# One attention and FFN layer in split fp32: joining the first score tiles of plain and latent keys in heads two to four of each group

## The chip, the cores and the metric

One core of one Trainium2 chip. The time is the device time of one execution of the whole program in microseconds; lower is better. TensorE is the matmul engine, VectorE, ScalarE and GpSimd work on tiles, and SyncE (SP) issues the transfers between the chip's memory (HBM) and the on-chip buffer SBUF. PSUM holds what TensorE writes.

## The reference

An attention layer and an FFN layer on an input x of shape (1, 1024, 512), both ahead of a residual addition and behind a layer norm:

```
q  = rope(x @ w_q)          # 32 heads of 128
k  = rope(x @ w_k)          # 8 key heads, each for 4 query heads
v  = x @ w_v                # 8
lk = rope((x @ w_lq) @ w_lk)   # 32 latent key heads, from a latent of 128
lv = x @ w_lv                  # 32
attn = causal_softmax(q @ k.T / sqrt(128)) @ v
lat  = causal_softmax(q @ lk.T / sqrt(128)) @ lv
x = x + attn @ w_o + lat @ w_lo
x = x + x_norm @ W.T + b + LoRA mixed by a router
```

Each head therefore has two attentions with the same queries: one over the plain keys of its group, one over latent keys of its own.

## The kernel before

All large products are made three times in a split form: each operand is kept as a rounded high part and the remainder (`hi` and `lo`), and `mm3` adds lo x hi, hi x lo and hi x hi into one PSUM tile. ScalarE makes the high part (a copy that rounds), VectorE or GpSimd the remainder (a subtraction).

The work is 8 groups (`g`) of 4 heads (`hh`, 0 to 3). A head has four passes `w`, in the order of `WINDOWS`: pass 0 is plain keys and queries 0 to 511 (chunk `c` = 0), pass 1 plain keys and queries 512 to 1023, pass 2 and pass 3 the same with latent keys. A pass with c = 0 has 4 blocks of 128 keys, one with c = 1 has 8. A block is a slot `s`. In each slot TensorE does, in this order:

- the score tiles of the NEXT pass whose place `TILE_SLOTS[w][t]` is this slot (tile `t` has 128 queries and all keys up to its diagonal, so 128 to 512 keys for c = 0 and 640 to 1024 for c = 1);
- a `piece` if `pieces_of` has one: a projection (Q and K of the next head or group, latent keys `LK`, latent values `LV`, values `V`) or a tile of the output projection (`OUT0`, `OUT1`);
- the transposes of the probabilities of block s + 2 into `bankT`, then the product of block s with the values into `bankO`.

In the last slot it also transposes blocks 0 and 1 of the next pass. The order on every engine is written out by hand, and semaphores tie the engines. A score tile goes TensorE (`scores[t % 2]`), VectorE (`row_max`, which adds the mask, writes the scaled scores to `probs` and their maximum to `nmax`), ScalarE (`exp_tile`, in place, with the row sum in `rsum`), TensorE (transposes). A transposed block goes through ScalarE (`block_hi`, L887) and VectorE (`block_lo`, L1113). TensorE may not overwrite a `scores` buffer before its row maximum is done, nor `bankT[j % 2]` before `block_lo` of the block in it (L580 to L582).

A rotary piece (Q, K, LK) is copied by ScalarE into one of three buffers `rot` (`rope_take`), multiplied by the sines on VectorE (`rotate`, two instructions of 64 partitions, L1123 and L1124), multiplied by the cosines and added on GpSimd (`rope_add`), rounded by ScalarE (`rope_high`), and its remainder made on GpSimd (`rope_low`). The latent keys of a head have two pieces, chunk 0 and chunk 1, both in pass 0 of that head, slots 0 and 1. Tile t = 0 of pass 2 is made in pass 1, slot 1, and waits for the remainder of chunk 0. Tiles t = 0 of pass 0 (next head) are made in pass 3, slot 4.

SP fetches weights through two staging buffers in turn; the load of number n waits for the remainder of weight n - 2. It also stores the inverse row sums and loads them back spread over the partitions (`spread_inverses`) between the weight loads.

Of the kernel before, what the change touches and what calls it, by code (L numbers as in the profile page):

```python
# [46 lines left out]
def pieces_of(g, hh, w):  # L47
# [3 lines left out]
    if w == 0:  # L51
        return {0: ("LK", 0), 1: ("LK", 1), **({3: ("LV", 0)} if more else {})}
    if w == 1:
        if (g, hh) == FIRST:
            return {0: ("LV", 1), 2: ("LV", 2), 5: ("LV", 3)}
        out = {s: ("OUT1", n) for n, s in enumerate((1, 2, 4, 7) if next_group else (1, 3, 5, 7))}
        ahead = {3: ("K", 0), 5: ("K", 1), 6: ("V", 0)} if next_group else {}
        return {**({0: ("LV", 1)} if more else {}), **out, **ahead}
# [18 lines left out]
def loads_of(g, hh):  # L77

    if (g, hh) == FINAL:
        return ["Wo", "Wlo"]  # L80
    if hh % 2:
        return (["Wk", "Wv"] if hh == GROUP - 1 else []) + ["Wq", "Wo", "Wlo", "Wlk"]
    if (g, hh) == (KVH - 1, GROUP - 2):
        return ["Wq", "Wo", "Wlo", "Wlk"]
    return ["Wq", "Wlv0", "Wo", "Wlo", "Wlk", "Wlv1"]


ROPE = ("Q", "K", "LK")
# [68 lines left out]
def attn_ffn_kernel(nc, x_in, w_q, w_k, w_v, w_o, w_lq, w_lk, w_lv, w_out_latent, W, b, A, B, router_W, router_b,  # L157
                    cos_in, sin_in, mask_in, ident_in, pick_in, out, inverses):
    with ExitStack() as ctx:
# [19 lines left out]
        KT = pair("KT", [P, S])  # L179
        LKT = pair("LKT", [P, S])  # L180
# [19 lines left out]
        nmax = sb("nmax", [P, 2, TPC])  # L200
        rsum = sb("rsum", [P, 2, TPC])
# [37 lines left out]
        Wlv0, Wlv1 = [[h[:, :, k * HD:(k + 1) * HD] for h in Wlv] for k in range(2)]  # L239

# [84 lines left out]
        def tiles_made(g, hh, w):  # L325

            return TPC * (unit_no(g, hh, w) + 1)
# [32 lines left out]
        def tile_bank(n, c, width):  # L360
            return scores[n % 2][:, 0, 0:width] if c == 0 else scores[n % 2][:, :, 0:width // 2]

# [37 lines left out]
        def _(sp):  # L400
# [39 lines left out]
            def group_of_heads(g, last):  # L440
                for hh in range(GROUP):
# [18 lines left out]
                    if more:  # L460
                        if hh == GROUP - 1:
                            fetch("Wk", "Wv", "Wq")
                        else:
                            fetch("Wq", "Wlv0" if "Wlv0" in loads_of(g, hh) else "Wo")
                    if not more:
# [10 lines left out]
                        sp.wait_ge(x_ready, n_piece(g, hh, 0, 0))  # L476
# [34 lines left out]
        def _(pe):  # L511
# [50 lines left out]
            def score_tile(no, parity, head, kind, c, t):  # L562

                if not (isinstance(no, int) and no < 2):
                    pe.wait_ge(row_maxed, no - 1)
# [3 lines left out]
                query = both(QT, ALL, head % 2, slice(i * P, (i + 1) * P))  # L569
                if c == 0:  # L570
# [7 lines left out]
            def transpose_block(g, hh, w, j):  # L578
# [4 lines left out]
                for t in range(max(0, j - TPC * c), TPC):  # L583
                    if j == 0:
                        pe.wait_ge(exped, tiles_made(g, hh, w) - TPC + t + 1)
                    at = p_offset(c, t) + j * P
                    mm = pe.transpose(bankT[j % 2][:, t * P:(t + 1) * P],  # L587
                                      probs[c][:, at:at + P], ident[:, :])
# [16 lines left out]
            def piece(g, hh, w, s, name, n):  # L605
                bank_x_taken(pe, g, hh, w, s)
                bank = piece_bank(g, hh, w, s)
                if name == "LK":
                    pe.wait_ge(w_lo, key_load(g, hh) + 1)
                    mm = mm3(bankX[:, :], both(Wlk, ALL, ALL), both(lqT, ALL, slice(n * CH, n * CH + CH)), True, True)  # L610
                elif name == "LV":
# [40 lines left out]
            def group_of_heads(g, last):  # L652
                for hh, w, more in windows(g, last):
# [8 lines left out]
                    for s in range(BLOCKS[w]):  # L662
                        if more or w < NW - 1:
                            for t in range(TPC):
                                if TILE_SLOTS[w][t] != s:
                                    continue
                                no = tiles_made(g, hh, w) + t
                                if t == 0 and w in (1, 2):

                                    pe.wait_ge(rope_lo, rope_no(g, hh, "LK", w - 1) + 1)  # L670
                                if t == 0 and w == 3:

                                    pe.wait_ge(rope_lo, rope_no(g, hh, "Q", 0) + 1)
                                if t == 0 and w == 0:

                                    pe.wait_ge(rope_lo, rope_no(g, hh, "LK", 0))
                                if t == 1 and w == 0:
                                    pe.wait_ge(x_free, frees_ahead(g, hh, 0))
                                if t == 1 and w == 2:
                                    pe.wait_ge(x_free, frees_ahead(g, hh, 2))  # L680
                                score_tile(no, t % 2, nhh, WINDOWS[nw][0], WINDOWS[nw][1], t)
# [45 lines left out]
            for t in range(TPC):  # L727
                if t == 1:
                    pe.wait_ge(x_free, 3)
                score_tile(t, t % 2, 0, 0, 0, t)  # L730
# [81 lines left out]
        def _(act):  # L812
# [60 lines left out]
            def exp_tile(no, c, t):  # L873

                act.wait_ge(row_maxed, no + 1)
                act.activation(prob_tile(c, t), prob_tile(c, t), ACT.Exp, bias=nmax[:, c, t:t + 1], scale=-1.0,  # L876
                               accum_out=rsum[:, c, t:t + 1]).then_inc(exped, 1)
# [12 lines left out]
            highs = [{(0, 3): ("LK", 0), (1, 0): ("LK", 1), (3, 1): ("Q", 0), (3, 3): ("Q", 1)} for _ in range(GROUP)]  # L890
            highs[GROUP - 1].update({(1, 5): ("K", 0), (2, 0): ("K", 1)})

            def group_of_heads(g, last):
                for hh, w, more in windows(g, last):
                    nw, nhh = (w + 1) % NW, hh + (w == NW - 1)
                    kind, c = WINDOWS[w]
                    for s in range(BLOCKS[w]):
# [4 lines left out]
                        early = s + 2 < BLOCKS[w] and name in ("", "LK", "OUT0", "OUT1")  # L902
                        if early:
                            block_hi(g, hh, w, s + 2)
                        if more or w < NW - 1:
                            for t in range(TPC):
                                if TILE_SLOTS[w][t] == s:
                                    exp_tile(tiles_made(g, hh, w) + t, WINDOWS[nw][1], t)
# [596 lines left out]
```

## Time and profile before

| | |
|---|---|
| Time, median of 3 runs | 2036.36 us (2036.19 to 2036.54) |
| Time of the profiled execution | 2036.75 us |
| Its span, first to last instruction | 2035.0 us |
| Busy: TensorE, VectorE, ScalarE, GpSimd | 2018.2, 1457.1, 1203.7, 889.9 us |
| Mean granted TensorE clock | 0.998 |

Busy time is the time in which at least one instruction of the engine runs. Matmuls overlap, so their durations add up to more than the span; the pace of TensorE is the distance between starts. The granted clock is 1.0 at full speed. A row of the order of time gives the start, the duration, the engine, the line, what is written and read and the shape, and in brackets the idle time before it with what ended it.

### The profile page before, as it was taken

To read this page: it belongs to the slowest core of one execution; us is meant where nothing else is said; L and a number is where in the kernel's file an instruction comes from. 1 tells how busy PE (TensorE), PEld (TensorE's weight loads), DVE (VectorE), ACT (ScalarE), POOL (GpSimd) and SP (SyncE) were. 2 spreads that over 40 slices of the span, in tenths; PEclk is the share of its full clock that TensorE was granted. 3 is DMA by queue.
4 is the path that set the end of the run, shared out by engine and by line. 5 is a ranking of instruction groups with operands and counts; after the bars stand their busy time and mean duration, and the time that the engine had idled before them with its cause. 6 is when DMAs were issued, how large, how long until landed. Compare 5 with 4: busy or idle time off the path is not lost.

```text
span 2035.0 us, 33416 instructions
## 1 busy us (share of the span) xinstructions
PE 2018.2 (99%) x11716; PEld 1753.1 (86%) x11716; DVE 1457.1 (72%) x2884; ACT 1203.7 (59%) x2505; POOL 889.9 (44%) x684
## 2 busy tenths in 40 slices
PE   8999999999999999999999999999999999999989
PEld 7888888888888888888888888888888888888877
DVE  7677776776777767777677776777776776777777
ACT  4666556565565656666566565666566565565651
POOL 5444544444443454444534454444544444443422
PEclk9999999999999999999999999999999999999999
DMA  3111111111111111112111111111111111111031
GB/s 108 47 34 44 48 28 38 34 49 37 38 39 39 33 44 37 44 28 49 33 44 37 39 39 28 49 34 44 48 28 41 32 49 39 37 39 38 23 68 42
DMA packets 101797, 83.78 MB, mean 41 GB/s; under 512 B 28152, under 2 KB 73848, under 8 KB 101632
## 3 DMA queue, kind: packets, MB, share of 16 engines
q1 hardware_dynamic: 101632, 81.65, 15.7%
q8 instruction: 95, 1.56, 0.3%
q14 instruction: 70, 0.57, 0.1%
HBM read 79.26 MB, written 2.36 MB: 40 GB/s over the span
## 4 chain that ended last, share of the span: by engine, by line
PE 97%; DVE 2%; ACT 1%; POOL 0%; issue 0%; DMA 0%; DVEq 0%; ACTq 0%
PE bankT L587 13%; PE scores L514 12%; PE scores L516 12%; PE scores L515 12%; PE bankX L514 9%; PE bankX L516 9%; PE bankX L515 9%; PE bankO L516 7%; PE bankO L515 7%; PE bankO L514 7%; PE scores L707 0%; PE scores L553 0%; DVE rot_half L1124 0%; DVE xnT_lo L1097 0%; ACT probs L876 0%
## 5 line engine op out<-in xcount | busy, mean ns | idle before, releaser
L815 ACT ACTIVATE PT_hi<-bankT 128x512 fp32r<-128x512 f32 (+2 forms) x640 | 337.5, 533 | 310.7 <-PE bankO L516 275.5
L1113 DVE TENSOR_TENSOR PT_lo<-bankT,PT_hi 128x512 fp32r<-128x512 f32 (+2 forms) x640 | 388.1, 607 | 175.7 <-ACT PT_hi L815 173.1
L876 ACT ACTIVATE probs<-probs,nmax 128x128 f32<-128x128 f32 (+7 forms) x512 | 393.9, 771 | 129.8 <-DVE nmax L1107 129.7
L1107 DVE CUSTOM_DVE_ANT_0 probs<-scores,mask 128x128 f32<-128x128 f32 (+7 forms) x512 | 379.2, 750 | 69.3 <-PE scores L516 68.0
L587 PE MATMUL bankT<-ident,probs 128*128 128x128 f32 x2304 | 382.7, 275 | 6.8 <-ACT probs L876 5.0
L587 PEld LDWEIGHTS bankT<-ident,probs 128*128 128x128 f32 x2304 | 279.6, 140 | 67.9 <-DVE PT_lo L1113 11.7
L1369 POOL TENSOR_TENSOR rot<-rot,cos 128x512 f32<-128x512 f32 x144 | 186.9, 1298 | 256.6 <-DVE rot_half L1124 256.6
L1363 POOL TENSOR_TENSOR OT_lo<-o_raw,OT_hi 128x512 fp32r<-128x512 f32 x63 | 98.3, 1560 | 319.9 <-ACT OT_hi L815 319.9
L815 ACT ACTIVATE OT_hi<-o_raw 128x512 fp32r<-128x512 f32 x128 | 146.7, 1146 | 139.7 <-DVE o_raw L1182 139.7
L1371 POOL TENSOR_TENSOR rot<-rot,rot_half 128x512 f32<-128x512 f32 x144 | 199.9, 1388 | 11.3
L1123 DVE TENSOR_TENSOR rot_half<-rot,sin 64x512 f32<-64x512 f32 x144 | 99.5, 691 | 135.3 <-ACT rot L815 132.3
L815 ACT ACTIVATE rot<-bankX 128x512 f32<-128x512 f32 x140 | 82.9, 592 | 101.9 <-PE bankX L516 101.9
L1124 DVE TENSOR_TENSOR rot_half<-rot,sin 64x512 f32<-64x512 f32 x144 | 140.6, 976 | 2.0
L514 PE MATMUL scores<-LKT_hi,QT_lo 128*128 128x384 f32 (+5 forms) x384 | 138.7, 361 | 0.2 <-POOL LKT_lo L1363 0.2
L1363 POOL TENSOR_TENSOR QT_lo<-rot,QT_hi 128x512 fp32r<-128x512 f32 x64 | 91.8, 1435 | 103.5 <-ACT QT_hi L815 103.5
L514 PE MATMUL bankO<-PT_hi,V_lo 128*128 128x512 f32 (+2 forms) x320 | 136.4, 426 | 0.0
L514 PE MATMUL bankO<-PT_hi,LV_lo 128*128 128x512 f32 (+2 forms) x320 | 136.2, 426 | 0.0
L1140 DVE TENSOR_TENSOR acc<-bankX,acc 128x512 f32<-128x512 f32 x133 | 91.7, 690 | 61.1 <-PE bankX L516 61.1
L514 PE MATMUL scores<-KT_hi,QT_lo 128*128 128x384 f32 (+5 forms) x384 | 133.0, 346 | 0.3 <-DVE nmax L1107 0.3
L516 PE MATMUL scores<-LKT_hi,QT_hi 128*128 128x384 f32 (+5 forms) x384 | 131.8, 343 | 0.0
L515 PE MATMUL scores<-LKT_lo,QT_hi 128*128 128x384 f32 (+5 forms) x384 | 131.5, 342 | 0.0
L516 PE MATMUL scores<-KT_hi,QT_hi 128*128 128x384 f32 (+5 forms) x384 | 131.4, 342 | 0.0
(304 smaller groups left out, 5334.0 us busy)
## 6 DMA issues: line engine op xcount, KB each, us to landing
inv_b<-inverses SPq DMA_DIRECT2D x128, 256.0 KB, 3.9
stage<-in_L_attn_w_q SPq DMA_DIRECT2D x32, 256.0 KB, 4.8
stage<-in_L_attn_w_lv SPq DMA_DIRECT2D x32, 256.0 KB, 2.9
stage<-in_L_attn_w_o SPq DMA_DIRECT2D x32, 256.0 KB, 3.5
stage<-in_L_attn_w_lo SPq DMA_DIRECT2D x32, 256.0 KB, 2.6
acc<-in_L_attn_hidden_states SPq DMA_DIRECT2D x8, 256.0 KB, 4.9
stage<-in_L_attn_w_k SPq DMA_DIRECT2D x8, 256.0 KB, 5.0
stage<-in_L_attn_w_v SPq DMA_DIRECT2D x8, 256.0 KB, 5.0
```

The costliest lines, as they stand in the source:

```text
L514: pe.matmul(place, left[1], right[0], start=start, stop=False)
L515: pe.matmul(place, left[0], right[1], start=False, stop=False)
L516: return pe.matmul(place, left[0], right[0], start=False, stop=stop)
L587: mm = pe.transpose(bankT[j % 2][:, t * P:(t + 1) * P], probs[c][:, at:at + P], ident[:, :])
L815: return act.activation(place, src, ACT.Copy)
L876: act.activation(prob_tile(c, t), prob_tile(c, t), ACT.Exp, bias=nmax[:, c, t:t + 1], scale=-1.0, accum_out=rsum[:, c, t:t + 1]).then_inc( ...
L1107: dve.tensor_tensor_reduce(place, src, tile_view(mask[:, S - width:S], c), -SCALE, -MASKED, ALU.add, ALU.min, nmax[:, c, t:t + 1]).then_in ...
L1113: dve.tensor_tensor(pt_place(1, hh, w, j), bankT[j % 2][:, block_columns(c, j):CH], f32(pt_place(0, hh, w, j)), ALU.subtract).then_inc(pt_ ...
L1124: dve.tensor_tensor(rot_half[HALF:HD, half, :], rot[0:HALF, slot, :], sin[0:HALF, t], ALU.mult)\
L1363: return pool.tensor_tensor(place, src, f32(hi), ALU.subtract)
L1369: pool.tensor_tensor(rot[:, slot, :], rot[:, slot, :], cos[:, chunk(n)], ALU.mult).then_inc(rope_cos, 1)
L1371: pool.tensor_tensor(rot[:, slot, :], rot[:, slot, :], rot_half[:, half, :], ALU.add).then_inc(rope_sum, 1)
```

## The change

In heads hh = 1, 2 and 3 of each group (24 of the 32 heads) the score tile t = 0 of pass 0 (plain keys) and tile t = 0 of pass 2 (latent keys) have the same queries, 0 to 127, and 128 keys each. They are now made in one `mm3` of 256 columns in pass 3, slot 4 of the head before. For this:

- plain and latent keys lie in one tensor `keys_T` of [128, 2, 1024], so that one operand can read 128 columns of each.
- the latent piece of chunk 0 is made one head ahead, as `LKA` in pass 1, slot 4 (hh = 0 to 2), from a weight `Wlk` that is loaded, rounded and split earlier (pass 1). Its rotation on VectorE comes two slots later, behind the row maximum of tile t = 3. ScalarE rounds it in pass 2, slot 0, after a wait for the last score tile that reads the old keys; GpSimd makes its remainder between those of `Wo` and `Wlo`.
- the row maximum and the exponential of the latent tile move with it; its probabilities lie in a tile of their own, `probs_ahead`, until pass 2, and its maxima and sums in a third set.
- head 0 of each group keeps both tiles and both pieces where they were.
- on GpSimd, the remainder of Q's chunk 0 in pass 3 now waits until VectorE has rotated Q's chunk 1.

```diff
     if w == 0:
-        return {0: ("LK", 0), 1: ("LK", 1), **({3: ("LV", 0)} if more else {})}
+        return {**({0: ("LK", 0)} if hh == 0 else {}), 1: ("LK", 1), **({3: ("LV", 0)} if more else {})}
...
+        latent = {4: ("LKA", 0)} if hh < GROUP - 1 else {}
+        return {**({0: ("LV", 1)} if more else {}), **out, **ahead, **latent}
...
-        return (["Wk", "Wv"] if hh == GROUP - 1 else []) + ["Wq", "Wo", "Wlo", "Wlk"]
+        return (["Wk", "Wv"] if hh == GROUP - 1 else []) + ["Wq", "Wlk", "Wo", "Wlo"]
...
-    return ["Wq", "Wlv0", "Wo", "Wlo", "Wlk", "Wlv1"]
+    return ["Wq", "Wlk", "Wlv0", "Wo", "Wlo", "Wlv1"]
...
+def tiles_at(g, hh, w, s):
+    if w == NW - 1 and (g, hh) == FINAL:
+        return []
+    to = (g, hh, w + 1) if w < NW - 1 else (*divmod(g * GROUP + hh + 1, GROUP), 0)
+    tiles = []
+    for t in range(TPC):
+        if TILE_SLOTS[w][t] == s:
+            if t or w != 1 or hh == 0:
+                tiles.append((*to, t))
+            if t == 0 and w == NW - 1 and to[1]:
+                tiles.append((*to[:2], 2, 0))
+    return tiles
...
-        KT = pair("KT", [P, S])
-        LKT = pair("LKT", [P, S])
+        keys_T = pair("keys_T", [P, 2, S])
...
+        KT, LKT = [[h[:, kind, :] for h in keys_T] for kind in range(2)]
...
# SP
-                            fetch("Wq", "Wlv0" if "Wlv0" in loads_of(g, hh) else "Wo")
+                            fetch("Wq", "Wlk")
...
-                    if hh == GROUP - 1 or "Wlv0" in loads_of(g, hh):
-                        fetch("Wo")
-                    fetch("Wlo")
+                    if hh == GROUP - 1:
+                        fetch("Wlk")
+                    if "Wlv0" in loads_of(g, hh):
+                        fetch("Wlv0")
+                    fetch("Wo", "Wlo")
                     spread_inverses(g, hh, 2)
-                    fetch("Wlk")
...
# TensorE, score_tile
+                if (w, t) == (0, 0) and hh:
+                    mm3(scores[0][:, 0, 0:2 * P].rearrange("p (k n) -> p k n", k=2), query,
+                        both(keys_T, ALL, ALL, slice(0, P)), True, True).then_inc(scored, 2)
+                    return
...
# ScalarE
+                        if w == 1 and s == (5 if hh == GROUP - 1 else 2) and more:
+                            act.wait_ge(x_ready, n_piece(g, hh, 0, 1))
+                            fetched(g, hh, "Wlk", Wlk)
...
+                            if s == 0 and hh < GROUP - 1:
+                                act.wait_ge(scored, tiles_made(g, hh, 3))
+                                rope_high(rope_no(g, hh, "LKA", 0), rope_no(g, hh, "LKA", 0) % RING, LKT[0][:, 0:CH])
...
-                        if w == 3 and s == 5 and more:
-                            fetched(g, hh, "Wlk", Wlk)
...
# VectorE
-                        if here.get(s - 1, ("", 0))[0] == "LK":
-                            piece(g, hh, w, s - 1, *here[s - 1], piece_bank(g, hh, w, s - 1))
+                        for behind_by, name in ((1, "LK"), (2, "LKA")):
+                            at = s - behind_by
+                            if here.get(at, ("", 0))[0] == name:
+                                piece(g, hh, w, at, *here[at], piece_bank(g, hh, w, at))
...
# GpSimd
                     if w == 1 and more:
                         fetched_low(g, hh, "Wq", Wq)
+                        if hh < GROUP - 1:
+                            fetched_low(g, hh, "Wlk", Wlk)
...
                             fetched_low(g, hh, "Wlv0", Wlv0)
+                        if hh < GROUP - 1:
+                            rope_add(rope_no(g, hh, "LKA", 0), rope_no(g, hh, "LKA", 0) % RING, 0)
...
                         fetched_low(g, hh, "Wo", Wo)
+                        if more and hh < GROUP - 1:
+                            rope_low(rope_no(g, hh, "LKA", 0), rope_no(g, hh, "LKA", 0) % RING, LKT, (ALL, chunk(0)))
                         fetched_low(g, hh, "Wlo", Wlo)
...
                     if w == 3 and more:
+                        pool.wait_ge(rope_half, rope_no(g, hh, "Q", 1) + 1)
                         rope_low(rope_no(g, hh, "Q", 0), rope_no(g, hh, "Q", 0) % RING, QT, q_at(0))
```

## Rows read from the trace of the kernel before

**Rows 1.** The page: busy time, share of the span and instructions of each engine.

```profile
PE 2018.2 (99%) x11716; PEld 1753.1 (86%) x11716; DVE 1457.1 (72%) x2884; ACT 1203.7 (59%) x2505; POOL 889.9 (44%) x684
```

**Rows 2.** The page: shares of the chain that ended last.

```profile
PE 97%; DVE 2%; ACT 1%; POOL 0%; issue 0%; DMA 0%; DVEq 0%; ACTq 0%
```

**Rows 3.** The waits, all engines: total us, times, longest.

```profile
PEld scores L514 <- POOL LKT_lo L1363: 11.6, 32, 0.9
```

**Rows 4.** Order of time, TensorE, pass 3, slots 3 and 4, around tile t = 0.

```profile
583.86 0.39 PE L516 MATMUL bankO<-PT_hi,LV_hi 128*128 128x512 f32 x1
...
584.54 0.28 PE L515 MATMUL scores<-KT_lo,QT_hi 128*128 128x256 f32 x1
584.66 0.28 PE L516 MATMUL scores<-KT_hi,QT_hi 128*128 128x256 f32 x1
```

**Rows 5.** Order of time, TensorE, pass 0, slot 0.

```profile
594.00 0.39 PE L514 MATMUL bankX<-lqT_hi,Wlk_lo 128*128 128x512 f32 x1
...
594.70 0.38 PE L587 MATMUL bankT<-ident,probs 128*128 128x128 f32 x2
```

**Rows 6.** Windows in the last head: us, busy (instructions), granted clock, DMA share, GB/s.

```profile
1938.00:1943.00 5.00, 1.44 (x10) 0.97 (x9) 4.23 (x6) 3.10 (x7) 4.16 (x3) 1.00 0.08 28
1943.00:1949.80 6.80, 6.48 (x21) 4.98 (x21) 4.19 (x9) 2.27 (x3) 3.86 (x4) 0.50 0.03 2
```

**Rows 7.** Order of time, TensorE, pass 1, slots 0 and 1.

```profile
608.79 0.40 PE L516 MATMUL bankO<-PT_hi,V_hi 128*128 128x512 f32 x1
...
609.10 0.33 PE L514 MATMUL scores<-LKT_hi,QT_lo 128*128 128x128 f32 x1
...
609.77 0.40 PE L515 MATMUL bankX<-Wo_lo,OT_hi 128*128 128x512 f32 x1
```

**Rows 8.** Order of time, GpSimd, ahead of the latent tile t = 0.

```profile
607.74 1.30 POOL L1363 TENSOR_TENSOR LKT_lo<-rot,LKT_hi 128x512 fp32r<-128x512 f32 x1
```

**Rows 9.** Order of time, VectorE, start of pass 0.

```profile
593.38 0.69 DVE L1113 TENSOR_TENSOR PT_lo<-bankT,PT_hi 128x512 fp32r<-128x512 f32 x1 [0.43 <-ACT PT_hi L815]
```

**Rows 10.** Order of time, VectorE, last head, pass 0.

```profile
1936.67 0.69 DVE L1123 TENSOR_TENSOR rot_half<-rot,sin 64x512 f32<-64x512 f32 x1
...
1938.09 1.22 DVE L1107 CUSTOM_DVE_ANT_0 probs<-scores,mask 128x1024 f32<-128x1024 f32 x1
```

**Rows 11.** Order of time, VectorE, end of pass 1, start of pass 2.

```profile
678.55 0.69 DVE L1107 CUSTOM_DVE_ANT_0 probs<-scores,mask 128x512 f32<-128x512 f32 x1 [0.59 <-PE scores L516]
...
680.12 0.69 DVE L1140 TENSOR_TENSOR acc<-scores,acc 128x512 f32<-128x512 f32 x1 [0.87 <-PE scores L516]
681.25 0.69 DVE L1113 TENSOR_TENSOR PT_lo<-bankT,PT_hi 128x512 fp32r<-128x512 f32 x1 [0.44 <-ACT PT_hi L815]
...
682.92 0.17 DVE L1200 RECIPROCAL rinv<-rsum 128x4 f32<-128x4 f32 x1
```

**Rows 12.** Order of time, TensorE, pass 2, tile t = 2.

```profile
683.86 0.48 PE L514 MATMUL scores<-LKT_hi,QT_lo 128*128 128x448 f32 x1
684.17 0.36 PE L515 MATMUL scores<-LKT_lo,QT_hi 128*128 128x448 f32 x1
```

**Rows 13.** Order of time, GpSimd, end of pass 1, the same head.

```profile
677.27 1.28 POOL L1363 TENSOR_TENSOR Wlv_lo<-stage,Wlv_hi 128x512 fp32r<-128x512 f32 x1 [4.04 <-ACT Wlv_hi L815]
```

**Rows 14.** Order of time, VectorE, pass 0, slot 2.

```profile
603.36 1.68 DVE L1124 TENSOR_TENSOR rot_half<-rot,sin 64x512 f32<-64x512 f32 x1
```

**Rows 15.** Order of time, GpSimd, the same moment.

```profile
602.81 1.67 POOL L1371 TENSOR_TENSOR rot<-rot,rot_half 128x512 f32<-128x512 f32 x1
```

**Rows 16.** Order of time, VectorE, start of the program.

```profile
16.77 0.38 DVE L1057 BATCH_NORM_AGGREGATE inv_b<-inv_b 128x2 f32<-128x6 f32 x4
17.18 0.89 DVE L1064 TENSOR_SCALAR inv_b<-inv_b 128x4 f32<-128x4 f32 x1
```

**Rows 17.** Order of time, GpSimd, the same moment.

```profile
16.75 1.29 POOL L1363 TENSOR_TENSOR Wlv_lo<-stage,Wlv_hi 128x512 fp32r<-128x512 f32 x1 [2.46 <-ACT Wlv_hi L815]
```

**Rows 18.** DMA issues: KB each, median us from issue to landing.

```profile
stage<-in_L_attn_w_lv SPq DMA_DIRECT2D x32, 256.0 KB, 2.9
```

More of the change, by code:

```diff
@@ L81, in loads_of, with number_tiles @@
     if hh % 2:
-        return (["Wk", "Wv"] if hh == GROUP - 1 else []) + ["Wq", "Wo", "Wlo", "Wlk"]
+        return (["Wk", "Wv"] if hh == GROUP - 1 else []) + ["Wq", "Wlk", "Wo", "Wlo"]
     if (g, hh) == (KVH - 1, GROUP - 2):
-        return ["Wq", "Wo", "Wlo", "Wlk"]
-    return ["Wq", "Wlv0", "Wo", "Wlo", "Wlk", "Wlv1"]
-ROPE = ("Q", "K", "LK")
+        return ["Wq", "Wlk", "Wo", "Wlo"]
+    return ["Wq", "Wlk", "Wlv0", "Wo", "Wlo", "Wlv1"]
[11 more added lines that the diff above has]
+    return tiles
+def number_tiles():
+    order = [(*FIRST, 0, t) for t in range(TPC)]
+    for g in range(KVH):
+        for hh in range(GROUP):
+            for w in range(NW):
+                for s in range(BLOCKS[w]):
+                    order += tiles_at(g, hh, w, s)
+    last, ahead = [None, None], {}
+    for at in order:
+        ahead[at] = last[at[3] % 2]
+        last[at[3] % 2] = at
+    return {at: no for no, at in enumerate(order)}, ahead
+TILE_NO, AHEAD_IN_SCORES = number_tiles()
+ROPE = ("Q", "K", "LK", "LKA")
 X_BEFORE = 10
@@ L610, in piece @@
                     mm = mm3(bankX[:, :], both(Wlk, ALL, ALL), both(lqT, ALL, slice(n * CH, n * CH + CH)), True, True)
+                elif name == "LKA":
+                    pe.wait_ge(w_lo, load_no(g, hh, "Wlk") + 1)
+                    mm = mm3(banksX[bank], both(Wlk, ALL, ALL), both(lqT, ALL, slice(0, CH)), True, True)
                 elif name == "LV":
@@ L901, in group_of_heads @@
                                       piece_bank(g, hh, w, s))
-                        early = s + 2 < BLOCKS[w] and name in ("", "LK", "OUT0", "OUT1")
+                        early = s + 2 < BLOCKS[w] and name in ("", "LK", "LKA", "OUT0", "OUT1")
                         if early:
                             block_hi(g, hh, w, s + 2)
[L905 to L908, printed above, removed]
-                        if name in ("Q", "K"):
+                        for at in tiles_at(g, hh, w, s):
+                            exp_tile(*at)
+                        if name in ("Q", "K", "LKA"):
                             rope_take(n_piece(g, hh, w, s), rope_no(g, hh, name, n), rope_no(g, hh, name, n) % RING,
@@ L1363, in subtract, with rope_add @@
                 return pool.tensor_tensor(place, src, f32(hi), ALU.subtract)
-            def rope_add(no, slot, n, place=None):
-                half = n if place is None else place
+            def rope_add(no, slot, n):
+                half = no % 2
                 pool.wait_ge(rope_half, no + 1)
@@ L1389, in ropes @@
             def ropes(g, hh, name, places, at):
-                for n in range(2):
+                halves = range(1 if hh and name == "LK" else 0, 2)
+                for n in halves:
                     rope_add(rope_no(g, hh, name, n), rope_no(g, hh, name, n) % RING, n)
-                for n in range(2):
+                for n in halves:
                     rope_low(rope_no(g, hh, name, n), rope_no(g, hh, name, n) % RING, places, at(n))
@@ L1421, in group_of_heads @@
                         rope_add(*k_no[1], 1)
+                        fetched_low(g, hh, "Wlk", Wlk)
                     if w == 1 and more:
```

116 lines of the change are left out of this document (61 added, 55 removed).

## Prediction

> **What bounds the kernel now.** I read the busy shares first, then the chain, then the waits, and then the order of instructions over one head. TensorE is busy 99% of the span and VectorE 72% [rows 1]; the chain that ended last is TensorE for 97% [rows 2]. So a change pays only by what it takes from TensorE's own stream, or from the gaps in it. Gaps are few. The one that this change touches is the weight load of the first latent score tile, which waits for LKT_lo in all 32 heads, 11.6 us in total [rows 3], mostly under the matmul that still runs. In the order of time the reader should look at the distance between starts, not at the durations, because matmuls overlap. A 256-column matmul advances by 0.115 us (584.54 to 584.66); the three 128-column ones before it by 0.11 each (0.68 from 583.86, less 0.23 for the matmul that starts there and 0.115) [rows 4]; a 512-column one advances by 0.23 us (594.00 to 594.70 is three) [rows 5]. A 128-column matmul is therefore paced by something other than its columns, and doubling the columns is nearly free. All of this is at a granted clock of 1.0; one stretch, in the last head, is at 0.5 [rows 6].
>
> **The sum, part by part.** The base is the profiled execution: span 2035.0 us, its time 2036.75, so 1.75 lie around the span; the median of the three runs is 2036.36, 0.39 below it. I subtract from the median.
>
> (a) The latent tile t = 0 leaves pass 1 in 24 heads. The last matmul ahead of it starts at 608.79, the second matmul behind it at 609.77 [rows 7]. Without the tile two steps of 0.23 us lie between: 0.46. The tile costs 0.98 - 0.46 = 0.52 us, its wait included. The wait: LKT_lo ends at 609.04 [rows 8] and the tile starts at 609.10.
>
> (b) The plain tile t = 0 becomes three 256-column matmuls. Before, 583.86 to the second matmul of t = 1 at 584.54 is 0.68 us [rows 4]. After: 0.23, three of 0.115 and one of 0.115 give 0.69. Cost 0.01. So (a) and (b) save 0.51 x 24 = 12.2 us. The trace has no operand in two runs of 128 columns; the bounds are 0 and a pace of twice 0.11, that is 3 x 0.105 = 0.32 us per head. I take 0, nearest to the 256-column rows, which differ in the stride alone. The Trainium skill ("TensorE: Matmul & The Clock Gate", Back-to-back issue gap) gives a warm gap of N/2.4 + 2.5 ns: 56 ns at 128 columns and 109 at 256. By that two tiles apart would cost as much as one joined tile, and the joining would save nothing; the trace's 0.11 us at 128 columns speaks against it.
>
> (c) The key piece of chunk 0 (three 512-column matmuls, 0.70 us [rows 5]) moves from pass 0 slot 0 to pass 1 slot 4 of the head before. The TensorE work is the same, but in pass 0 it was cover. Behind it stands the transpose group that overwrites bankT0, and it waits for PT_lo, which runs from 593.38 for 0.69, to 594.07 [rows 9]. TensorE would now come to it at 594.00 instead of 594.70. A start 0.06 behind the releaser (as 609.10 behind 609.04) is 594.13, so 0.13 late. The tile of (a) shows that a wait costs somewhat more than its late start: 0.52 us for three steps of 0.11 leaves 0.19, though it started only 0.08 late (609.10 against 608.79 + 0.23). I take 0.16 us in 24 heads: 3.8 us lost; bounds 0 and 0.25.
>
> (d) VectorE. The rotation of the moved piece (two instructions of 0.69 [rows 10]) goes behind the last row maximum of pass 1. There VectorE is free from 679.25 until 680.12 [rows 11]. Rotation 679.28 to 680.70, the addition of the output tile until 681.31 (0.61 from start to start), so PT_lo starts 0.06 late against 681.25. From there everything to the row maximum of the next pass is back to back, and TensorE's tile t = 2 already waits for that: its first step takes 0.31 us (683.86 to 684.17) where a 448-column step, between those of 256 and 512 columns, takes some 0.2 [rows 12]. So 0.06 x 24 = 1.4 us lost. In the 15 heads that round both a moved piece and a value half Wlv0 in pass 1, GpSimd's Wlv_lo now starts later; before it ended at 678.55 [rows 13], 0.7 us ahead of where the rotation would begin. ScalarE takes the new piece first (0.6 us) and TensorE puts it 0.2 later, so in a count with that shift it ends about 679.45, and the rotation starts at 679.49. I add 0.05 x 15 = 0.8; bounds 0 and 1.0 each. The added row maximum and exponential of 128 columns only move from pass 1 to pass 3 slot 4, where VectorE and ScalarE wait for TensorE.
>
> (e) GpSimd's multiplication and addition for the moved piece (1.3 us each) now run from about 680.8 to 683.5, over the reciprocal at 682.92 [rows 11], which reads and writes SBUF. What can be held? A rotation on VectorE took 1.68 instead of 0.69 us while a GpSimd addition ran to 604.48 [rows 14, 15]; a 4-element TENSOR_SCALAR from 17.18 took 0.89 us and ended with GpSimd's instruction at 18.04, but four BATCH_NORM_AGGREGATE beside the same one took 0.38 together [rows 16, 17]. No reciprocal in the trace overlaps one. Bounds: 0, or held to about 683.46, which is some 0.35 us for the row maximum and for TensorE behind it. I take 0. The Trainium skill ("SBUF — State Buffer", Who interferes with whom) has two-input instructions from SBUF and copy, cast and tensor_scalar as those that contend with GpSimd; the rows agree for the first and the last, and it does not name the reciprocal.
>
> (f) New waits. GpSimd waits for the second rotation of Q before QT_lo, about 0.6 us later, but then runs 1.3 instead of 1.7 us, done near 583.6 against about 584.1 for the tile (0.23 behind 583.86 [rows 4]): nothing. ScalarE waits in pass 2 for the last score tile, then rounds the keys (0.64 us); its next instruction needed a transpose behind that tile anyway, and the last exponential moves by 0.6 us where 1 us was free: nothing; beyond that, each tenth costs 2.4 us. The Wlk load moves ahead on SP, and its rounding (0.3) and GpSimd's remainder (0.5) into pass 1; the first latent value half and both output weights load one place later. They land some 3 us after issue (the value half's row [rows 18]) and are used 5 us later or more, except Wlv0, in (d). Nothing.
>
> (g) The last head. There is no other work on TensorE between passes, so it stands still behind the exponentials. Its 1,024-column row maximum stood behind the rotation of chunk 0 (1936.67, maximum at 1938.09), then PT_lo of the next pass behind a second rotation and ScalarE's rounding of the same keys [rows 10]. Without them the maximum starts 1.0 us earlier, and the transposes that ended the standstill near 1943.2 start near 1941.4: 1.8, of which 0.6 is already in (c). Add 0.4 for the longer wait at the latent tile. 1.6 us gained. Then the clock: granted 0.50 for 6.8 us from 1943.0, behind five us in which it was busy for 1.44 [rows 6]. TensorE now waits about 2.5 us in all there. I take it that the clock stays at 2.4 GHz; what it gives back is half of 6.8 less about 1.4 us of waits, 2.7 us. Bounds 0 and 2.7.
>
> Sum: -12.2 + 3.8 + 1.4 + 0.8 - 1.6 - 2.7 = -10.5 us: 2036.36 - 10.5 = 2025.9, say **2026** (with the clock down, 2028.6).
>
> **Rivals.** *The reciprocal is held* (e): 24 x 0.35 = +8.4, 2034.3: no measurable change. For it the TENSOR_SCALAR, against it the BATCH_NORM_AGGREGATE. *The joined tile is no cheaper* (b): 24 x 0.32 = +7.7, 2033.6. For it only that such an operand is nowhere in the trace. *The rotation meets Wlv_lo* (d), which ends on the other side: if that GpSimd instruction starts a few tenths later, or if the load of Wlv0 lands late, the rotation is held for its whole length, 1.0 us, and PT_lo and the row maximum with it, in 15 heads: +15, 2041. It cancels the gain from 0.7 us in each of them and is measurably slower from 1.0, its whole price. For it: the gap that I work out is 0.04 us. Against it: a small overlap costs only itself, and SP can issue this load some 7 us before use. *Other cover is lost* ((c) and (f) at their upper bounds, a tenth or two in 24 heads): 2031 to 2036.
>
> **How the numbers follow.** A measurement tells this kernel from itself within about 0.2%, 4.1 us. Forecast 0.62 (its own range 2022 to 2031), all faster; a gain above it 0.05, if (c) and (d) cost nothing (2020); reciprocal 0.11 and joined tile 0.04, no change; lost cover 0.09, split 0.04 faster and 0.05 no change; rotation 0.09 (with a little of the other losses beside it, which its whole price needs), 0.08 slower and 0.01 no change. Faster 0.71, same 0.21, slower 0.08. For eight in ten I leave out what lies under 2020.5 and over 2036.5.
>
> **What the profile after would show.** 72 joined matmuls of 256 columns at a pace of 0.115 us; no LKT tile of 128 columns in those heads; a wait of the transposes for PT_lo in pass 0 of some 0.15 us in 24 heads; the step of t = 2 in pass 2 at 0.35 to 0.4 us; a reciprocal of 0.17 us; one rotation in pass 1 of 0.69 twice; a clock of 1.0 near the end. The distance from head to head should shrink by about 0.3 us. Wrong would be a reciprocal or a rotation of over 1 us there, or a wait for QT_lo or exponentials that is not there now.

## The result, and the profile after

The changed kernel takes 2044.47 us (median of 6 runs, 2042.87 to 2045.78); the kernel before, on the same chip, 2036.28 (2035.65 to 2036.54). The ratio is 1.0038, with a 95% interval of 1.0028 to 1.0048: slower by 8.2 us, where 10.5 us less were forecast. The profiled execution has a span of 2044.0 us against 2035.0. Its own time is 2045.78, the slowest of the six, so what follows explains 9.0 us where the medians differ by 8.2.

The page of the changed kernel: busy time by engine, the chain that ended last (its line is quoted whole), and the one group that is new among the costliest.

```profile
PE 2021.3 (99%) x11644; PEld 1747.7 (86%) x11644; DVE 1432.6 (70%) x2884; ACT 1206.3 (59%) x2505; POOL 871.1 (43%) x684
...
PE 97%; DVE 2%; issue 0%; ACT 0%; DMA 0%; SPq 0%; DVEq 0%; ACTq 0%
PE scores L559 12%; PE bankT L637 12%; PE scores L561 12%; PE scores L560 12%; PE bankX L559 9%; PE bankX L561 9%; PE bankX L560 9%; PE bankO L561 7%; PE bankO L559 7%; PE bankO L560 7%; DVE o_raw L1242 1%; PE scores L598 0%; ACT probs L931 0%; DMA stage<-in_L_attn_w_q 0%; DVE probs L1149 0%
...
L559 PE MATMUL bankO<-PT_hi,V_lo 128*128 128x512 f32 (+2 forms) x320 | 136.4, 426 | 6.0 <-DVE o_raw L1242 6.0
```

72 matmuls are gone [rows 1], and TensorE is still busy 99% of the span. Busy time alone would have hidden the loss. What is new is VectorE's o_raw (line 1242) in the chain, and idle time of TensorE ahead of the first product with V. Its waits say the same (total us, times, longest); in the kernel before there is no wait of TensorE for o_raw at all, and the wait for the latent keys had 11.6 us in 32 places [rows 3].

```profile
PEld bankT L637 <- DVE PT_lo L1173: 16.0, 50, 1.0
PEld scores L559 <- POOL keys_T_lo L1423: 2.8, 8, 0.4
PE bankO L559 <- DVE o_raw L1242: 6.0, 24, 0.3
```

**The loss in pass 0.** The order of time in slot 0 of pass 0, second head of a group (start, duration; PE is TensorE, DVE VectorE), in the changed kernel:

```profile
597.76 0.69 DVE L1173 TENSOR_TENSOR PT_lo<-bankT,PT_hi 128x512 fp32r<-128x512 f32 x1 [0.44 <-ACT PT_hi L870]
598.24 0.31 PE L561 MATMUL scores<-keys_T_hi,QT_hi 128*128 128x320 f32 x1
598.37 0.68 DVE L1242 TENSOR_TENSOR o_raw<-bankO,inv_b 128x512 f32<-128x512 f32 x1
598.51 0.44 PE L637 MATMUL bankT<-ident,probs 128*128 128x128 f32 x2
599.20 0.47 PE L559 MATMUL bankO<-PT_hi,V_lo 128*128 128x512 f32 x1 [0.25 <-DVE o_raw L1242]
```

and the two rows of the kernel before that answer to the third and the fifth (the transposes are in [rows 5]):

```profile
593.99 0.68 DVE L1182 TENSOR_TENSOR o_raw<-bankO,inv_b 128x512 f32<-128x512 f32 x1
...
594.83 0.48 PE L514 MATMUL bankO<-PT_hi,V_lo 128*128 128x512 f32 x1
```

The transposes were due 0.15 us behind the score matmul of 598.24 and start 0.12 later than that; by the ends it is 0.18 (598.95 is 0.40 behind the end of the score matmul at 598.55; before, 595.08 was 0.22 behind the end of the key piece at 594.86): the wait that the forecast had. Then comes a second one. The product overwrites bankO, which o_raw reads until 599.05. Before, o_raw ended at 594.67, when the key piece was just running out, and the product ended 0.23 us behind the transposes (595.31 against 595.08). Now it ends 0.72 behind them (599.67 against 598.95): 0.49 us of standstill. The moved piece had covered two waits, not one.

**The loss in pass 3.** TensorE's first product with Wo, in slot 2, needs OT_lo. It ends 0.47 us behind the end of the matmul ahead of it, in the kernel before 0.31, where the pace is 0.23. The cause lies 6 us earlier, in the order of time of all engines (ACT is ScalarE, POOL GpSimd):

```profile
633.29 0.63 ACT L870 ACTIVATE keys_T_hi<-rot 128x512 fp32r<-128x512 f32 x1
...
636.15 0.62 ACT L870 ACTIVATE Wlo_hi<-stage 128x512 fp32r<-128x512 f32 x1
636.84 1.28 POOL L1423 TENSOR_TENSOR Wlo_lo<-stage,Wlo_hi 128x512 fp32r<-128x512 f32 x1 [1.06 <-ACT Wlo_hi L870]
637.78 0.89 DVE L1183 TENSOR_TENSOR rot_half<-rot,sin 64x512 f32<-64x512 f32 x1 [2.90 <-ACT rot L870]
...
641.97 1.08 DVE L1250 TENSOR_TENSOR OT_lo<-o_raw,OT_hi 128x512 fp32r<-128x512 f32 x1 [0.69 <-ACT OT_hi L870]
642.80 0.40 PE L561 MATMUL bankO<-PT_hi,LV_hi 128*128 128x512 f32 x1
643.20 0.47 PE L559 MATMUL scores<-Wo_hi,OT_lo 128*128 128x512 f32 x1
```

The rounding of the moved keys stands on ScalarE ahead of the last two exponentials, these end later, and with them Wlo_hi and Wlo_lo. Wlo_lo now runs until 638.12, over the start of VectorE's rotation of Q, which takes 0.89 us. Before, Wlo_lo ended at 633.23, just as the rotation began, and the rotation took 0.69:

```profile
631.95 1.28 POOL L1363 TENSOR_TENSOR Wlo_lo<-stage,Wlo_hi 128x512 fp32r<-128x512 f32 x1 [1.98 <-ACT Wlo_hi L815]
633.17 0.69 DVE L1123 TENSOR_TENSOR rot_half<-rot,sin 64x512 f32<-64x512 f32 x1 [2.90 <-ACT rot L815]
...
638.17 0.40 PE L516 MATMUL bankO<-PT_hi,LV_hi 128*128 128x512 f32 x1
638.41 0.47 PE L514 MATMUL scores<-Wo_hi,OT_lo 128*128 128x512 f32 x1
```

PT_lo, o_raw, ScalarE's OT_hi and OT_lo follow the rotation one behind the other, so the 0.2 us arrive at the product.

**The books.** For every matmul I take the distance of its end from the end of the one ahead, less the usual distance for its width, and add up by place over 23 of the 24 heads, scaled to 24. In us:

| part | forecast | profile |
|---|---|---|
| latent tile gone, tiles joined | -12.2 | -11.7 |
| transposes wait for PT_lo, pass 0 | +3.8 | +4.5 |
| product with V waits for o_raw, pass 0 | not seen | +11.7 |
| first product with Wo, pass 3 | 0 | +5.1 |
| tile t = 2 of pass 2; Wlv_lo | +2.2 | +1.1 |
| last head: standstill and clock | -4.3 | -2.5 |
| start of the program | 0 | +0.8 |
| sum | -10.5 | +9.0 |

The spans differ by 9.0. What makes the last row but one is not shown. In this execution the clock was at 0.50 for 3.4 us from 15.9, which it was not in the execution of before; but the profiled execution of e10, with the same drop, ends its 251st matmul at 53.02 against 52.92 before, and that of e2, without a drop, at 53.55.

### The profile page after: what moved, and what is told of

Read it like the earlier page. It is cut to its first block, busy times and chain, and to the rows that moved or that the text cites. A ratio compares the mean times of both kernels' runs of the same rounds, so it can differ in the third digit from the quotient of the medians.

```text
span 2044.0 us, 33310 instructions
## 1 busy us (share of the span) xinstructions
PE 2021.3 (99%) x11644; PEld 1747.7 (86%) x11644; DVE 1432.6 (70%) x2884; ACT 1206.3 (59%) x2505; POOL 871.1 (43%) x684
## 4 chain that ended last, share of the span: by engine, by line
PE 97%; DVE 2%; issue 0%; ACT 0%; DMA 0%; SPq 0%; DVEq 0%; ACTq 0%
PE scores L559 12%; PE bankT L637 12%; PE scores L561 12%; PE scores L560 12%; PE bankX L559 9%; PE bankX L561 9%; PE bankX L560 9%; PE bankO L561 7%; PE bankO L559 7%; PE bankO L560 7%; DVE o_raw L1242 1%; PE scores L598 0%; ACT probs L931 0%; DMA stage<-in_L_attn_w_q 0%; DVE probs L1149 0%
## 5 line engine op out<-in xcount | busy, mean ns | idle before, releaser
L931 ACT ACTIVATE probs<-probs,nmax 128x256 f32<-128x256 f32 (+7 forms) x480 | 380.8, 796 | 120.4 <-DVE nmax L1167 120.2
L1167 DVE CUSTOM_DVE_ANT_0 probs<-scores,mask 128x256 f32<-128x256 f32 (+7 forms) x480 | 371.8, 781 | 100.0 <-PE scores L561 99.6
L559 PE MATMUL scores<-keys_T_hi,QT_lo 128*128 128x384 f32 (+5 forms) x744 | 264.0, 355 | 0.3 <-DVE nmax L1167 0.3
L561 PE MATMUL scores<-keys_T_hi,QT_hi 128*128 128x384 f32 (+5 forms) x744 | 256.4, 345 | 0.0
L560 PE MATMUL scores<-keys_T_lo,QT_hi 128*128 128x384 f32 (+5 forms) x744 | 256.3, 344 | 0.0
L1183 DVE TENSOR_TENSOR rot_half<-rot,sin 64x512 f32<-64x512 f32 x144 | 104.2, 723 | 135.8 <-ACT rot L870 132.8
L559 PEld LDWEIGHTS scores<-keys_T_hi,QT_lo 128*128 128x128 f32 x744 | 139.9, 188 | 24.7 <-DVE nmax L1167 10.4
L1423 POOL TENSOR_TENSOR keys_T_lo<-rot,keys_T_hi 128x512 fp32r<-128x512 f32 x80 | 103.6, 1294 | 125.9 <-ACT keys_T_hi L870 125.9
L560 PEld LDWEIGHTS scores<-keys_T_lo,QT_hi 128*128 128x128 f32 x744 | 140.0, 188 | 11.9
L561 PEld LDWEIGHTS scores<-keys_T_hi,QT_hi 128*128 128x128 f32 x744 | 139.7, 188 | 10.1
```

The costliest lines, as they stand in the source:

```text
L559: pe.matmul(place, left[1], right[0], start=start, stop=False)
L560: pe.matmul(place, left[0], right[1], start=False, stop=False)
L561: return pe.matmul(place, left[0], right[0], start=False, stop=stop)
L931: act.activation(tile_of(w, t), tile_of(w, t), ACT.Exp, bias=nmax[:, exp_sums(w), t:t + 1], scale=-1.0, accum_out=rsum[:, exp_sums(w), t:t ...
L1167: dve.tensor_tensor_reduce(place, src, tile_view(mask[:, S - width:S], c), -SCALE, -MASKED, ALU.add, ALU.min, nmax[:, exp_sums(w), t:t + 1 ...
L1183: dve.tensor_tensor(rot_half[0:HALF, half, :], rot[HALF:HD, slot, :], sin[HALF:HD, t], ALU.mult)
```

## Experiments

Each kernel is timed against the kernel before on its chip (2036.32, 2036.58 and 2036.88 us in the three groups); all stand beside the changed kernel's 2044.47. The changed kernel was not run again on those chips; the kernel before differs between them and its first chip (2036.28) by up to 0.6 us, so a difference of that size between groups says nothing. Of each edit the main lines are shown.

**e1_cover_back.** The key piece of chunk 1 moves from slot 1 to slot 0.

```diff
-        return {**({0: ("LK", 0)} if hh == 0 else {}), 1: ("LK", 1), **({3: ("LV", 0)} if more else {})}
+        keys = {0: ("LK", 1)} if hh else {0: ("LK", 0), 1: ("LK", 1)}
+        return {**keys, **({3: ("LV", 0)} if more else {})}
```

Not shown: four waits of SP and ScalarE for the last piece of pass 0 that follow it to its new place.

> The changed kernel, but in heads two to four of a group the one key piece that is left in pass 0 (chunk 1, three 512-column matmuls, 0.70 us) goes to slot 0 instead of slot 1. Theory A (lost cover): in the changed kernel TensorE stands still twice in slot 0 of pass 0, about 0.18 us for PT_lo ahead of the transposes and about 0.49 us ahead of the first product with V, which waits for o_raw to read out bankO. A piece in between covers both: 0.67 x 24 = 16 us less than the changed kernel's 2044.5, so 2028 to 2029, the wait for o_raw gone from the waits, and about 8 us less than the kernel before. Rival B (the loss lies in VectorE's and ScalarE's later work, the keys' rounding and rotation, and the stall in slot 0 only shows it): the time stays at 2042 to 2045, and the idle time turns up again ahead of the tiles of slot 1 or of the product in slot 1, which now lack the piece. Rival C (only half is covered, since slot 1 needs the piece as well): about 2036.

Measured: 2033.65 us (10 runs), ratio to before 0.9987 (0.9977 to 0.9996), 10.8 less than the changed kernel. Both waits are gone: in the order of time the piece starts at 595.37, the transposes at 596.06 and the product at 596.20, and the waits show none for o_raw. But a gain of 16 us was expected. One wait has grown: that of the transposes for the probabilities had 6.4 us in 7 places in the changed kernel and now has 11.0 in 30, while the one for PT_lo went from 16.0 in 50 to 10.5 in 26.

```profile
PEld bankT L638 <- ACT probs L932: 11.0, 30, 2.9
PEld bankT L638 <- DVE PT_lo L1174: 10.5, 26, 0.7
```

The order of time at the end of the pass shows where.

```profile
600.94 0.69 DVE L1184 TENSOR_TENSOR rot_half<-rot,sin 64x512 f32<-64x512 f32 x1
601.64 0.69 DVE L1185 TENSOR_TENSOR rot_half<-rot,sin 64x512 f32<-64x512 f32 x1
602.36 1.23 DVE L1168 CUSTOM_DVE_ANT_0 probs<-scores,mask 128x1024 f32<-128x1024 f32 x1
603.63 1.15 ACT L932 ACTIVATE probs<-probs,nmax 128x1024 f32<-128x1024 f32 x1 [1.75 <-DVE nmax L1168]
604.50 0.75 PE L638 MATMUL bankT<-ident,probs 128*128 128x128 f32 x4
```

Four transposes usually take 0.60 us to the last end. Here 0.75: the last waits for the exponential that ends at 604.78. The rotation came ahead of the row maximum again, and TensorE, with one piece less in this pass, is now faster than that chain. Theory A holds for the waits of slot 0; a part of the gain went to a wait that had been hidden (rival C in kind, but at the end of the pass, not in slot 1).

**e5_rotation_behind.** The same, with that rotation behind the row maximum.

```diff
-                        for behind_by, name in ((1, "LK"), (2, "LKA")):
+                        for behind_by, name in ((2 if hh else 1, "LK"), (2, "LKA")):
```

> The kernel with the cover back (chunk 1 in slot 0), and VectorE rotates that piece behind the row maximum of the fourth tile instead of ahead of it, in heads two to four. With the cover back that row maximum started at the end of the rotation, its exponential ended at 604.78 and TensorE's transposes of the next pass waited 0.15 us for it in each of 24 heads. Theory A: the last 3.5 us go, 2033.65 - 3.5 = about 2030. Rival: the sum of the moved keys on GpSimd comes later and holds something of VectorE instead, so nothing or a loss: 2033.5 or above.

Measured: 2028.26 us, ratio 0.9958 (0.9943 to 0.9973). That is 5.4 less than e1, where 3.5 were expected; the distances between matmul ends give 3.5 for the transposes, and the last head is 0.7 us shorter. The rest, about a microsecond, lies behind the last head, where the profiled execution of e1 is 1.4 us longer than this one. There e1 has a drop of the clock that this execution has not (window, busy by engine, granted clock, DMA share, GB/s):

```profile
1968.20:1971.60 3.40, 3.40 (x14) 3.00 (x15) 2.71 (x5) 2.23 (x3) 0.00 (x0) 0.50 0.00 0
```

From the start of one group of transposes to that of the next, the stretch takes 3.69 us in e1 (from 1968.11) and 2.34 at a clock of 1.0 here (from 1963.46). Why the clock falls there in the one and not in the other is open. So the cover, with nothing put in its place, is worth 16.2 us, with 1.5 to either side by the spread of the four runs: the whole 4.5 + 11.7 of the table.

**e8_piece_twice** and **e10_before_twice.** Work is added instead of moved: in slot 0 of pass 0 TensorE computes a key piece once more, 0.70 us, in the changed kernel (chunk 1) and as a control in the kernel before (chunk 0, `slice(0, CH)`, bank of slot 0).

```diff
+                        if (w, s) == (0, 0) and hh:
+                            bank_x_taken(pe, g, hh, 0, 1)
+                            pe.wait_ge(w_lo, key_load(g, hh) + 1)
+                            mm3(bankX[:, :], both(Wlk, ALL, ALL), both(lqT, ALL, slice(CH, S)), True, True)
```

> The changed kernel with work added: in slot 0 of pass 0 of heads two to four TensorE computes the key piece of chunk 1 once more (three 512-column matmuls, 0.70 us; the result is computed again in slot 1, where it is used). Theory A (TensorE stands still there for 0.18 + 0.49 us): the added work is free but for 0.03 us a head, so 2044 to 2046. Rival (the stall is not idle time of TensorE, or comes back elsewhere): 0.70 x 24 = 17 us more, 2061.

> The control for the piece computed twice: the kernel before the change, with its key piece of chunk 0 computed once more in slot 0 of pass 0 of heads two to four (three 512-column matmuls, 0.70 us). In that kernel TensorE does not stand still there, so theory A says the same added work that was free in the changed kernel costs its whole 0.70 x 24 = 17 us: 2053. Rival (such work is free in this place in any kernel, and proves nothing of a stall made by the change): 2037 to 2040.

Measured: 2044.69 us in the changed kernel, 0.2 more than without the added work (and 8.1 above the kernel before on its own chip, as against 8.2); 2053.65 in the kernel before, 16.8 more than its 2036.88 (ratio 1.0084, 1.0068 to 1.0099). The same 72 matmuls are free in the one and cost their whole 0.70 us a head in the other. This is the plainest evidence that TensorE stood still there for about 0.67 us in 24 heads, and only since the change. In the order of time the product now starts 0.14 us behind the transposes, as before the change:

```profile
597.85 0.39 PE L561 MATMUL bankX<-lqT_hi,Wlk_hi 128*128 128x512 f32 x1
598.08 0.38 PE L637 MATMUL bankT<-ident,probs 128*128 128x128 f32 x2
598.22 0.48 PE L559 MATMUL bankO<-PT_hi,V_lo 128*128 128x512 f32 x1
```

**e2_keys_later.** The rounding of the moved keys goes behind the weights: on ScalarE behind the first two blocks of pass 3, on GpSimd behind the sum of Q.

```diff
                     if w == 2 and more:
                         rope_add(rope_no(g, hh, "Q", 0), rope_no(g, hh, "Q", 0) % RING, 0)
+                        if hh < GROUP - 1:
+                            rope_low(rope_no(g, hh, "LKA", 0), rope_no(g, hh, "LKA", 0) % RING, LKT, (ALL, chunk(0)))
```

Not shown: the lines that take both roundings out of pass 2, and ScalarE's new ones.

> The changed kernel, but the high and low rounding of the moved keys (ScalarE, then GpSimd, chunk 0) goes from between the weights of pass 2 to behind them: on ScalarE behind the first two PT_hi of pass 3, on GpSimd behind the sum of Q's chunk 0. Theory A: in the changed kernel that rounding pushes Wlo_lo under the rotation of Q, which takes 0.89 instead of 0.69 us, and everything behind is late, until TensorE's first product with Wo in pass 3 waits about 0.24 instead of 0.08 us for OT_lo. The edit takes back 0.16 x 24 = 4 us: about 2040.5. Rival B: nothing, since the rounding's GpSimd part now lies beside VectorE's OT_lo and holds it, or the wait in pass 3 has another cause: 2044 or above, with OT_lo longer than 1.1 us.

Measured: 2047.52 us, 3.0 more. Rival B was right about the time, not about the way. The product with Wo has its pace back (it starts 0.24 us behind the matmul ahead). The loss is one slot later:

```profile
642.11 1.09 DVE L1250 TENSOR_TENSOR OT_lo<-o_raw,OT_hi 128x512 fp32r<-128x512 f32 x1 [0.67 <-ACT OT_hi L870]
642.22 2.10 POOL L1423 TENSOR_TENSOR keys_T_lo<-rot,keys_T_hi 128x512 fp32r<-128x512 f32 x1
643.90 0.97 DVE L1183 TENSOR_TENSOR rot_half<-rot,sin 64x512 f32<-64x512 f32 x1
644.88 0.68 DVE L1184 TENSOR_TENSOR rot_half<-rot,sin 64x512 f32<-64x512 f32 x1
...
646.35 0.55 PE L637 MATMUL bankT<-ident,probs 128*128 128x128 f32 x3 [0.24 <-DVE PT_lo L1173]
```

OT_lo is not held (1.09 us, as ever). GpSimd is, for 2.10 us instead of 1.29, and so reaches into the next rotation, which takes 0.97; the transposes wait for the PT_lo behind it.

**e3_both.** e1 and e2 together.

> Both edits together. If the two losses are separate places on TensorE's path, they add up: 16 + 4 = 20 us less than the changed kernel, about 2024.5, and 12 us (0.6%) less than the kernel before, which is about what the forecast gave for the change without its losses. If the stall in slot 0 of pass 0 only took over slack, the sum is smaller than its parts: 2028 or above.

Measured: 2035.16 us (10 runs), where 2024.5 were expected, and 1.5 more than e1 alone. The loss of e2 comes back beside the gain of e1, so it says only what e2 says.

**e6_wlo_ahead.** The second try at pass 3: nothing is moved on GpSimd, but ScalarE rounds Wlo ahead of the last exponential of pass 2.

```diff
                         for at in tiles_at(g, hh, w, s):
+                            if at[2:] == (3, 3):
+                                fetched(g, hh, "Wlo", Wlo)
                             exp_tile(*at)
```

Not shown: the lines that take this rounding away from its place behind the exponential.

> The changed kernel, but on ScalarE the rounding of Wlo in pass 2 stands ahead of the last exponential instead of behind it, so that GpSimd computes Wlo_lo from about 635.8 to 637.1, before VectorE's rotation of Q begins at 637.8; the moved keys stay where the change put them. Theory A (Wlo_lo under the rotation is what makes OT_lo late): TensorE's first product with Wo in pass 3 waits 0.08 again instead of 0.24 us, 0.16 x 24 = 4 us less, about 2040.5. Rival: the last exponential comes 0.6 us later and the transposes behind Q's projection wait for it instead: 2044 or above.

Measured: 2040.70 us (10 runs), 3.8 less, as expected. Wlo_lo ends at 635.51, and the rotation takes 0.69 again:

```profile
634.21 1.30 POOL L1424 TENSOR_TENSOR Wlo_lo<-stage,Wlo_hi 128x512 fp32r<-128x512 f32 x1
...
636.25 0.69 DVE L1184 TENSOR_TENSOR rot_half<-rot,sin 64x512 f32<-64x512 f32 x1 [2.90 <-ACT rot L870]
```

By the distances between ends the first product with Wo gets back 0.21 us a head, 5.0 in all, which is the whole row of the table; the last head of this execution is 0.4 us longer, and the spans differ by 4.6.

**e4_tiles_apart.** The joined tile as two tiles of 128 columns at the same place.

```diff
-                    mm3(scores[0][:, 0, 0:2 * P].rearrange("p (k n) -> p k n", k=2), query,
-                        both(keys_T, ALL, ALL, slice(0, P)), True, True).then_inc(scored, 2)
+                    for k in range(2):
+                        mm = mm3(scores[0][:, 0, k * P:(k + 1) * P], query,
+                            both(keys_T, ALL, k, slice(0, P)), True, True)
+                    mm.then_inc(scored, 2)
```

> The changed kernel with the joined tile undone alone: at the same place six matmuls of 128 columns instead of three of 256. By the pace read before (0.11 us for 128 columns, 0.115 for 256) that is 6 x 0.11 - 3 x 0.115 = 0.315 us a head, 7.6 us over 24 heads: about 2052, so the joining itself pays as forecast. If the rule holds that 128 columns are paced by their columns (half of 256), the time stays within a microsecond of 2044.5.

Measured: 2051.99 us, 7.5 more than the changed kernel: 0.31 us a head, where 0.315 was worked out. The idea of the change is sound, and its size as forecast.

**e7_all_three.** e5 and e6 together.

> Cover back, rotation behind the row maximum and Wlo ahead, together. If the three losses lie in separate places and nothing else is lost, 2044.5 - 11 - 3.5 - 4 = 2026, 0.5% less than before, which is what the forecast gave for the change. If they share slack: 2029 or above.

Measured: 2024.66 us, ratio to before 0.9943 (0.9928 to 0.9958); 19.8 less than the changed kernel, and 16.2 + 3.8 = 20.0 by the parts. The losses are separate, and this is the version to keep: 0.57% faster than the kernel before.

**e9_no_wait_for_q.** e7 without GpSimd's new wait for the second rotation of Q.

> The kernel with all three repairs, 2024.7 us, without the change's new wait on GpSimd (in pass 3, for the second rotation of Q ahead of QT_lo). The forecast put that wait at nothing. Theory A (it costs nothing and gives nothing): 2024 to 2026, QT_lo takes 1.7 instead of 1.3 us under VectorE's rotation. Rival B (the wait is needed now): QT_lo starts as soon as ScalarE's QT_hi is done, which is just ahead of the second half of that rotation, holds it, and the transposes of pass 3 slot 3 wait for PT_lo as they did when the keys' remainder lay there (0.28 us in the mean over 24 heads): up to 7 us more, 2031. Rival C: it was a cost, and the time falls under 2023.

Measured: 2024.35 us, 0.3 less than e7, within what their runs differ: the wait costs nothing and gives nothing. Rival B fails by 0.14 us. QT_lo starts at 637.51, just behind the second half of the rotation (637.37), which keeps its 0.69, and GpSimd alone pays:

```profile
637.51 1.70 POOL L1425 TENSOR_TENSOR QT_lo<-rot,QT_hi 128x512 fp32r<-128x512 f32 x1 [2.47 <-ACT QT_hi L871]
```

## Why the forecast was wrong, step by step

**(c), the step that failed.** "In pass 0 it was cover" was right, and the wait for PT_lo was sized well: 4.5 us for 3.8. But the step asked only what stands directly behind the removed piece. The next instruction, the product of block 0, waits for o_raw to release bankO, and o_raw starts on VectorE only as PT_lo ends. Of the 0.70 us of cover that went, the first wait showed 0.18 and the second 0.49. That is 11.7 us in 24 heads; e5, e8 and e10 show it from three sides. No rival had it: "other cover is lost" reached only to 2036.

**(f), priced at nothing.** ScalarE's added rounding was judged by whether ScalarE could afford it, and it could. Not followed was what stands behind the displaced Wlo_hi: GpSimd's Wlo_lo, which before had ended as the rotation of Q began, with nothing to spare. 5.1 us by the distances, 3.8 by e6. The rival with the right mechanism, GpSimd under a rotation, was looked for in pass 1 and not in pass 2. The other waits of (f) were rightly nothing: the one for Q by e9 (taken out of e7, not of the changed kernel), and QT_lo (586.66, for 1.29 us) ends at 587.95, ahead of the tile at 588.42.

**(a) and (b), right.** -11.7 for -12.2. The six matmuls of joined tile and second tile start 0.12 us apart:

```profile
588.42 0.28 PE L559 MATMUL scores<-keys_T_hi,QT_lo 128*128 128x256 f32 x1
588.54 0.28 PE L560 MATMUL scores<-keys_T_lo,QT_hi 128*128 128x256 f32 x1
588.66 0.28 PE L561 MATMUL scores<-keys_T_hi,QT_hi 128*128 128x256 f32 x1
...
589.14 0.40 PE L559 MATMUL bankX<-Wo_hi,OT_lo 128*128 128x512 f32 x1
```

The two runs of 128 columns in the operand cost nothing that shows. The rival that the tile is no cheaper is out by e4. What the prediction took from the Trainium skill ("TensorE: Matmul & The Clock Gate", Back-to-back issue gap) it took wrongly: N/2.4 + 2.5 ns is there the gap of an isolated matmul, and the page says itself that this is too little at small N, where a stream of weight loads and matmuls has about 81 ns for 128 columns. By the formula e4 would have lost next to nothing; it lost 7.5 us, and its 128-column fp32r matmuls have a pace of 0.11 us, more than either figure.

**(d), right in kind, half the size.** The tile t = 2 is 1.1 us later in sum, for 1.4; the 0.8 for Wlv_lo and the rival that the rotation meets it did not come. In every head the rotation of the moved piece takes 0.68 or 0.69 twice, and where a Wlv_lo stands ahead of it in pass 1 (as in the third head of this group), that ends 0.21 to 0.22 us before the rotation starts, where the forecast had worked out 0.04:

```profile
682.78 1.30 POOL L1423 TENSOR_TENSOR Wlv_lo<-stage,Wlv_hi 128x512 fp32r<-128x512 f32 x1 [4.78 <-ACT Wlv_hi L870]
...
684.30 0.69 DVE L1183 TENSOR_TENSOR rot_half<-rot,sin 64x512 f32<-64x512 f32 x1
```

**(e), right.** The reciprocal is not held in any head. In the second head of the group GpSimd adds from 628.58 to 629.87, and

```profile
628.58 1.29 POOL L1431 TENSOR_TENSOR rot<-rot,rot_half 128x512 f32<-128x512 f32 x1
...
629.43 0.16 DVE L1260 RECIPROCAL rinv<-rsum 128x4 f32<-128x4 f32 x1
```

**(g), half right.** The last head is shorter, but the clock did fall, for 3.4 us instead of 6.8 [rows 6], behind five us in which TensorE was busy for 2.42. Windows (us, busy by engine, granted clock, DMA share, GB/s):

```profile
1949.65:1954.65 5.00, 2.42 (x18) 1.67 (x16) 3.86 (x7) 3.14 (x6) 2.07 (x2) 1.00 0.13 51
1954.65:1958.05 3.40, 3.39 (x10) 2.58 (x9) 2.49 (x5) 2.26 (x3) 0.86 (x2) 0.50 0.01 0
```

In sum: 11.7 unseen, 5.1 priced at nothing, and 2.7 in the small terms make the 19.5 us between -10.5 and +9.0. Open is what the start of the program adds, and why the clock falls there in some executions and not in others (in the changed kernel, e1 and e10, but not in the kernel before or the other experiments); no run was made to settle it.

## What to carry to other kernels

Before a piece of work is moved off the bounding engine's path, list not the first wait behind it but every wait until the next piece of free work, with the time at which each releaser ends: cover is used by all of them. When an instruction is put into another engine's queue, follow the displaced ones through every engine to where their results meet something that is tight; slack on the engine itself is no answer. And an experiment that adds idle work at the suspected place, with the same addition to the kernel before as a control, tells a standstill from a story in two runs.

## What the runs showed of the hardware

When a VectorE instruction with both inputs in SBUF (a rotation or OT_lo) and one of GpSimd overlapped, the one that started second paid. With GpSimd ahead (Wlo_lo from 636.84, the rotation from 637.78) VectorE took 0.89 us for 0.69. With VectorE ahead by 0.11 to 0.14 us it kept its 1.09 or 0.69, and GpSimd took 2.10 (e2) or 1.70 (e9) for 1.29. So the same overlap is free or costs the path by which of the two begins first.

The price was the overlap less a fixed part, whichever engine paid. With a rotation as the partner the fixed part is 0.14 us: an overlap of 0.34 cost 0.20 (Wlo_lo and the rotation, in all 24 heads), one of 0.42 cost 0.28 (e2) and one of 0.55 cost 0.41 (e9), while the 0.06 of the kernel before cost nothing. With OT_lo it is 0.17 in the rows of e2 (0.98 cost 0.81).

VectorE's PT_lo, which takes one input from PSUM, was not held: it took 0.67 to 0.69 us in all 189 places of the changed kernel in which a GpSimd instruction was running as it began (128x512). The 128 reciprocals of line 1260 (128x4 elements) took 154 to 189 ns, and those wholly under a GpSimd instruction 0.16 to 0.17 us.
